# Last stage: the signs of two pairs of units are added on GpSimd, and three engines' orders are changed

## The reference, cut to what matters

```python
# h: 16384 tokens x 64; weight (1, 8, 64, 64), proj_w (8, 64), scale (1, 1, 64)
xh   = layernorm(h)
gate = (sigmoid(xh @ proj_w.T + proj_b) > 0.5)        # 8 gates, 0 or 1, per token
w    = einsum('hbe,heio->hbio', gate, weight)         # a 64 x 64 matrix per token
y    = einsum('hbi,hbio->hbo', sign(xh), sign(w))     # sum over i of sign * sign
out  = h + y * scale
```

## Time and profile before

| | |
|---|---|
| median of three runs | 1976.49 us |
| the profiled execution's own time | 1986.12 us |
| its span | 1984.3 us |
| PE busy | 1697.9 us (86%) |
| DVE busy | 1182.7 us (60%) |
| ACT busy | 975.5 us (49%) |
| POOL busy | 422.9 us (21%) |
| last stage, first sign to the end | about 1192 to 1984.3 us |

### The profile page before, as it was taken

The page is one execution under the profiler, slowest core; times in us unless marked ns, Lnnn a source line. Parts: engine busy times, 40 slices in busy tenths (PEclk is TensorE's granted clock), DMA queues, the critical chain, the costliest instruction groups (busy, mean ns, idle before and its releaser), DMA issues.

```text
span 1984.3 us, 94332 instructions
## 1 busy us (share of the span) xinstructions
PE 1697.9 (86%) x35690; PEld 1234.3 (62%) x35690; DVE 1182.7 (60%) x3445; ACT 975.5 (49%) x1765; POOL 422.9 (21%) x477
## 2 busy tenths in 40 slices
PE   5999999956568888888888779999999999999996
PEld 3566666644457666666667556666666666666663
DVE  2565656567624444444444467777777777777762
ACT  2344444423312222222222227777777777777776
POOL 2100000034322332323323222222222222222210
PEclk9899999978979999999999969999999999999998
DMA  3100000125533333333333212333333333333332
GB/s 106 36 11 13 11 11 13 32 57 104 102 86 93 92 96 94 93 96 91 97 96 92 63 33 74 79 79 79 79 79 79 79 79 79 79 79 79 79 78 57
DMA packets 254173, 141.71 MB, mean 71 GB/s; under 512 B 181314, under 2 KB 218050, under 8 KB 253858
## 3 DMA queue, kind: packets, MB, share of 16 engines
q1 hardware_dynamic: 254114, 140.88, 29.5%
HBM read 63.56 MB, written 18.42 MB: 41 GB/s over the span
## 4 chain that ended last, share of the span: by engine, by line
issue 33%; PE 29%; SPq 26%; ACT 6%; DVE 2%; DMA 2%; POOL 1%; ACTq 0%; DVEq 0%; POOLq 0%
SPq L402 13%; PE ps_D L805 8%; SPq L391 4%; ACT prob L1060 3%; PE ps_AV L822 3%; SPq L373 2%; PE ps_J L859 2%; PE ps_J L911 2%; PE ps_OT L929 2%; PE ps_J L879 2%; SPq L428 1%; PE ps_J L937 1%; PE ps_OT L954 1%; SPq L394 1%; PE ps_OT L953 1%
## 5 line engine op out<-in xcount | busy, mean ns | idle before, releaser
L1060 ACT ACTIVATE prob<-ps_D 128x1024 bf16<-128x1024 f32 x448 | 443.6, 1022 | 83.6 <-PE ps_D L805 83.2
L1231 DVE TENSOR_REDUCE m_sb<-ps_D 128x4 f32<-128x400 f32 x256 | 135.4, 571 | 207.7 <-PE ps_D L708 192.1
L1048 ACT ACTIVATE prob<-ps_D 100x512 f32<-100x512 f32 x256 | 139.0, 595 | 216.8 <-PE ps_D L730 216.8
L493 POOL TENSOR_TENSOR tile_a<-q_st,q_mask 128x1024 f32<-128x1024 f32 x64 | 123.3, 1927 | 407.5 <-DMA q_st<-q_d 369.5
L730 PE MATMUL ps_D<-tile_a,key_patch 64*100 64x128 f32 x2048 | 176.7, 288 | 0.0
L726 PE MATMUL ps_D<-mT,key_rows 64*100 64x128 bf16 x1024 | 129.3, 224 | 51.0 <-ACT mT L1037 32.2
L1184 DVE TENSOR_REDUCE top<-ps_D 128x8 f32<-128x512 f32 x128 | 79.5, 684 | 152.5 <-PE ps_D L582 152.5
L805 PE MATMUL ps_D<-tile_b,w_parts 128*128 128x256 bf16 x1024 | 155.5, 275 | 15.5 <-ACT prob L1060 9.6
L805 PE MATMUL ps_D<-tile_a,w_parts 128*128 128x256 bf16 x1024 | 156.1, 276 | 14.2 <-ACT prob L1060 9.6
L730 PEld LDWEIGHTS ps_D<-tile_a,key_patch 64*100 64x100 f32 x2048 | 146.8, 166 | 0.0
L805 PEld LDWEIGHTS ps_D<-tile_a,w_parts 128*128 128x128 bf16 x1024 | 88.5, 100 | 60.3 <-issue 47.8
(11 more groups left out here) (174 smaller groups left out, 3880.9 us busy)
## 6 DMA issues: line engine op xcount, KB each, us to landing
tile_b<-v_d SPq DMA_DIRECT2D x640, 40.0 KB
tile_a<-xg SPq DMA_DIRECT2D x384, 64.0 KB, 2.0
tile_b<-xg SPq DMA_DIRECT2D x384, 64.0 KB, 2.0
key_st<-k_d SPq DMA_DIRECT2D x64, 175.0 KB, 3.0
key_st<-k_d SPq DMA_DIRECT2D x64, 167.0 KB, 3.1
w_exp<-experts SPq DMA_DIRECT2D x64, 129.0 KB, 2.3
k_d<-kpad SPq DMA_DIRECT2D x32, 140.0 KB, 2.3
xin<-in_x SPq DMA_DIRECT2D x32, 128.0 KB, 2.3
```

The costliest lines, as they stand in the source:

```text
L493: gp.tensor_tensor(q_block[:, par, :].rearrange("c (p h q) -> c p h q", h=NH, q=NQ), q_st[:, :].rearrange("c (p a q) -> c p a q", a=1, q=N ...
L1048: act.activation(prob1[0:NKL, 2 * g + x, :], s_loc[x][0:NKL, :], ACT.Exp).then_inc(T2["exp_done"], 1)
L1060: act.activation(sgn[:, k % 4, :], unit(k, par)[:, :], ACT.Sign).then_inc(BN["sign"], 1)
L1231: dve.tensor_reduce(m_sb[:, C * x + HOT[x] + 4 * g:C * x + HOT[x] + 4 * g + 4], m_loc[x][:, 0:4 * NKL].rearrange("p (u n) -> p u n", u=4), ...
```

## The change

For each strip, POOL now adds the signs of units 2 and 3 ("fold 1") and of units 4 and 5 ("fold 2") into a new bf16 tile `fold`, and PE sums the two folded tiles in place of the four, so it sums six tiles in place of eight. Sums of two signs are -2 to 2, exact in bf16. The folds stand on POOL behind the bias addition and ahead of `rstd_ret`. The waits follow: signs 6 and 7 wait for fold 1 (they overwrite slots 2 and 3), sign 0 and the clip of the next strip wait for fold 2.

The orders change too. On PE, reduce 1 stands behind w 6, reduce 2 behind w 1 of the next pass, ahead of reduce 3, and w 3 stands ahead of L859. On ACT, sign 2 stands ahead of the first ReLU, sign 3 ahead of the second. On DVE, the clip stands first in the pass, and `ud` and `ys` stand ahead of the `xn_fg` normalisations.

```diff
@@ gpsimd, strips(j, par), between the bias addition and inv_std("ret", RT, f)
+                if q is not None:
+                    for pair in (1, 2):
+                        gp.wait_ge(BN["sign"], times(q * 7 + 2 * pair + 1))
+                        gp.wait_ge(BN["y_part"], times(q * 4 - 3 + pair))
+                        settle(gp)
+                        two = [sgn[:, k % 4, :] for k in (2 * pair, 2 * pair + 1)]
+                        gp.tensor_tensor(fold[:, pair - 1, :], two[0], two[1], ALU.add).then_inc(BN["fold"], 1)
@@ tensor, reduce(q, pair)
-                    signed(q, 2 * pair + 1)
+                    if pair in (1, 2):
+                        pe.wait_ge(BN["fold"], times(q * 2 + pair))
+                        parts = [(fold[:, pair - 1, :], 0)]
+                    else:
+                        signed(q, 2 * pair + 1)
+                        parts = [(sgn[:, k % 4, :], int(k == 1)) for k in (2 * pair, 2 * pair + 1)]
@@ tensor, order
+                    reduce(p, 2)
                     reduce(p, 3)
...
+                if q is not None:
+                    signed(q, 1)
+                    weights(3, par, unit(3, par))
...
-                    signed(q, 1)
-                    weights(3, par, unit(3, par))
                     pe.wait_ge(BN["ysum"], times(q))
                     reduce(q, 0)
...
                     weights(5, par, unit(5, par))
-                    reduce(q, 1)
...
                     weights(6, par, unit(6, par))
-                    reduce(q, 2)
+                    reduce(q, 1)
@@ scalar, sign(k)
-                    act.wait_ge(BN["y_part"], times(q * 4 + k // 2 - 1))
+                    if k in (0, 6, 7):
+                        act.wait_ge(BN["fold"], times(q * 2 + (1 if k else 0)))
+                    else:
+                        act.wait_ge(BN["y_part"], times(q * 4 + k // 4))
@@ vector, the clip, now first in the pass
-                    dve.wait_ge(BN["y_part"], times(q * 4 - 1))
+                    dve.wait_ge(BN["fold"], times(q * 2))
```

More of the change, by code:

```diff
@@ L181, in build @@
         sgn = prob1[:, :, :].bitcast(BF16)
+        fold = sb("fold", [P, 2, 1024], BF16)
         x_parts = [tile_a[:, :, :].rearrange("p a n -> p (a n)").bitcast(BF16), tile_b[:, :, :].rearrange("p a n -> p (a n)").bitcast(BF16)]
@@ L231, in build @@
         BN = named("bin", "stats", "mv", "veps", "rstd", "xn", "xs", "g_ps", "gates", "x_ps", "xg", "x_in", "w_ps", "sign", "clip",
-                   "y_part", "ysum", "y_ps", "ys", "y", "stored")
+                   "fold", "y_part", "ysum", "y_ps", "ys", "y", "stored")
         CREDIT = 4
@@ L511, in strips @@
             def strips(j, par):
-                e, f, b = (inside(j - k) for k in (0, 1, 3))
+                e, f, b, q = (inside(j - k) for k in (0, 1, 3, 6))
                 if b is not None:
@@ L817, in reduce @@
                         signed(q, 0)
-                    signed(q, 2 * pair + 1)
+                    if pair in (1, 2):
[4 more added lines that the diff above has]
+                        parts = [(sgn[:, k % 4, :], int(k == 1)) for k in (2 * pair, 2 * pair + 1)]
                     settle(pe)
-                    for k in (2 * pair, 2 * pair + 1):
+                    for n, (part, by) in enumerate(parts):
                         for cg in range(4):
-                            mm = pe.matmul(bank["AV"][32 * cg:32 * (cg + 1), 0:256], lane_sum[:, int(k == 1), :], sgn[:, k % 4, cg * 256:(cg + 1) * 256],
-                                           start=k == 0, stop=k == 7)
+                            mm = pe.matmul(bank["AV"][32 * cg:32 * (cg + 1), 0:256], lane_sum[:, by, :], part[:, cg * 256:(cg + 1) * 256],
+                                           start=pair == 0 and n == 0, stop=pair == 3 and n == 1)
                     mm.then_inc(BN["y_part"], 1)
@@ L1073, in strips @@
                     act.activation(xs[:, :], bank["T"][:, 0:256], ACT.Sign).then_inc(BN["xs"], 1)
+                if q is not None:
+                    sign(2)
                 if f is not None:
@@ L1077, in strips @@
                     act.activation(hidT[:, 0, :], bank["J1"][:, 0:256], ACT.Relu, bias=b_i[:, 0:1]).then_inc(FF["hid_sb"], 1)
-                if q is not None:
-                    sign(2)
                 if r is not None:
@@ L1083, in strips @@
                     act.activation(xrT[:, :], bank["OT"][:, 0:256], ACT.Copy).then_inc(RT["xT_sb"], 1)
+                if q is not None:
+                    sign(3)
                 if f is not None:
@@ L1088, in strips @@
                 if q is not None:
-                    sign(3)
                     sign(4)
@@ L1297, in strips @@
                 turns = min(max(j, 0), NSTRIP + 3) if isinstance(j, int) else j
+                if q is not None:
+                    dve.wait_ge(BN["w_ps"], times(q * 8 + 2))
+                    dve.wait_ge(BN["fold"], times(q * 2))
+                    dve.tensor_scalar(sgn[:, 1, :], unit(1, par)[:, :], -TINY, TINY, ALU.max, ALU.min).then_inc(BN["clip"], 1)
                 if r is not None:
@@ L1303, in strips @@
                     dve.tensor_scalar(kd3[:, 1, 0:C + 1], xn_r[:, 1, 0:C + 1], decay_k[:, :], keep[:, 0, bass.ds(r, 1)], ALU.mult, ALU.mult).then_inc(RT["kd"], 1)
-                if q is not None:
-                    dve.wait_ge(BN["w_ps"], times(q * 8 + 2))
-                    dve.wait_ge(BN["y_part"], times(q * 4 - 1))
-                    dve.tensor_scalar(sgn[:, 1, :], unit(1, par)[:, :], -TINY, TINY, ALU.max, ALU.min).then_inc(BN["clip"], 1)
                 if g is not None:
@@ L1319, in strips @@
                     moments("ffn", FF, e, row(e * 2))
-                if e is not None:
-                    normalize("ffn", FF, e, row(e * 2), lambda t: xn_fg[:, t, 0:C], FF["xT_ps"], turns)
-                if b is not None:
-                    normalize("bin", BN, b, row(b * 2), lambda t: xn_fg[:, t, C:P], FF["xT_ps"], turns)
                 if r is not None:
@@ L1333, in strips @@
                                       scale_bc[:, :].rearrange("p (a c) -> p a c", a=1).broadcast_to((P, 2, C)), ALU.mult).then_inc(BN["ys"], 1)
+                if e is not None:
+                    normalize("ffn", FF, e, row(e * 2), lambda t: xn_fg[:, t, 0:C], FF["xT_ps"], turns)
+                if b is not None:
+                    normalize("bin", BN, b, row(b * 2), lambda t: xn_fg[:, t, C:P], FF["xT_ps"], turns)
                 if g is not None:
```

## The result

The changed kernel takes 1997.32 us at the median (1993.13 to 1999.31). The kernel before, run beside it, takes 1978.38 us (1973.61 to 1981.2). The ratio is 1.0103 [1.0086, 1.012]: slower by about 20 us, where +10 was forecast. The profiled execution took 1996.97 us (span 1994.8). That of before was 8 us above its median, so the two spans differ by only 10.5 us; the last stage, from the start of its first `xg` to the end, went from 808.6 us (1175.7 to 1984.3) to 828.9 us (1165.9 to 1994.8), 20.3 us more. (Counted from the first sign it is 21.9 us, but the new order of ACT puts that sign 1.6 us nearer to the first `xg`.)

The account below looks back on a forecast made before the run. PE was taken to bound the kernel before, fold 1's loop the changed one: 12.60 us per pass against 12.43, +0.17 over 58 passes, +9.9 us, so 1986.5 us. The forecast's own range was 1975 to 2003, the stated range 1942 to 2010 us.

Parts of the forecast that it names:

- the loop closed by fold 1: PE's first FFN layer (W), DVE chain, POOL's fold 1, signs 6 and 7, w 1, next W: 12.60 us per pass.
- w 1 to W: On PE, from w 1 to the next first FFN layer, with the clip and w 3 between: 2.54 us.
- the ends of the stage: First six passes without folds and last ones without bias addition: put at 0, with 3 us to either side.
- W to fold 1's start: First FFN layer on PE, through gates, moments, `xn_fg` and bias addition, to POOL's fold 1: 5.72 us.
- D: Length of a fold on POOL, 2.1 us, low end 1.1; also the rival that the change moves nothing, within 4 us.
- fold 1's end to w 1: Sign 6 starts 0.10 after fold 1, w 1 2.08 after sign 6's start, and `yo`'s hold adds about 0.05.
- The fewer matmuls: On PE, two tiles fewer to sum save 0.33 us per pass, 21 us over 64 strips if PE alone counted.
- PE's list: PE's own work without late folds: 6.29 us from W to w 6, 11.62 us per pass.
- the hold: DVE's `yo`, with two SBUF inputs, waits inside fold 1 until W + 7.97; adds about 0.05 us per pass.
- A: Rival: PE gets its gain, as a fold takes only 1.1 to 1.5 us; 1930 to 1948 us, chance 0.20.
- B: Rival: the walk is too strict, the loop's constant is 0.3 to 0.5 us smaller; 1963 us, chance 0.15.
- C: Rival: DVE's `yo` loses to both folds on POOL, a pass takes 14.75 us; 2110 us, chance 0.10.

Follow-up runs that it names:

- e2: The changed kernel with each fold adding only 512 of 1024 columns, PE reading these twice: 1943.87 us, 0.9848 of the kernel before.
- e3: The changed kernel with `yo` reading the unscaled sums from PSUM, so one SBUF input, scale left out: 1988.10 us, 1.0069 of the kernel before.
- e4: The changed kernel with `ud` and `ys` between the two `xn_fg` on DVE: 2147.84 us, 1.0872 of the kernel before.
- e1: The changed kernel without folds, PE summing eight tiles, reduces 1 and 2 behind w 5 and w 6: 1967.14 us, 0.9962 of the kernel before.
- e12: The kernel before with only DVE's gates moved behind the retention layer's addition and both moments: 1960.26 us, 0.9915 of the kernel before.
- e8: The changed kernel with DVE's gates behind the moments and both `xn_fg` ahead of `ud` and `ys`: 1952.17 us, 0.9867 of the kernel before.
- e9: e8's order on DVE without folds, PE summing eight tiles: 1949.94 us, 0.9872 of the kernel before.
- e11: The changed kernel with DVE's gates behind the moments, `ud` still ahead of `xn_fg`, `ys` behind it, folds kept: 1954.26 us, 0.9881 of the kernel before.

## Why the prediction was right or wrong

The direction was right, the forecast's range of 1975 to 2003 us held the time, and the mechanism forecast is the one seen: the loop closed by fold 1. The size was too small, +10 us for about +20. Two terms of the sum were mis-sized: the pass, 12.60 for 12.73, most of it in the step from w 1 to W (2.54 for 2.64), and the ends of the stage, put at 0, which cost about 4 us. Term by term, two successive passes, the first from W = 1500.81 and the second from 1513.50:

| step | forecast | pass 1 | pass 2 |
|---|---|---|---|
| W to fold 1's start | 5.72 | 5.66 | 5.79 |
| D | 2.10 | 2.125 | 2.125 |
| fold 1's end to w 1 | 2.23 | 2.27 | 2.25 |
| w 1 to W | 2.54 | 2.64 | 2.65 |
| sum | 12.59 | 12.69 | 12.81 |

- **The fewer matmuls** were priced rightly: two folded tiles cost 0.23 and 0.12, which saves 0.31 of the 0.66 of reduces 1 and 2 (forecast 0.33), and under the fold's loop they are worth nothing, as forecast. PE's list had 6.29 to w 6 and took 6.44, but that is two errors that nearly cancel. The stop at L889, below, is not in the 6.29 (reduce 0 to the transpose takes 0.92, 1501.44 to 1502.36, and took 0.35 before). Against it, PE lost more before than the idle in brackets says: w 5 came 0.47 behind the start of L901 (1509.52 to 1509.99) and comes 0.06 behind the start of L917 now (1504.47 to 1504.53), so its wait was worth 0.41 and not 0.25.
- **D** was taken from the f32 rows, 2.1, and measured 2.125. e2 shows what the low end of 1.1 would have given.
- **Fold 2** was to hold sign 0 back by 0.2 to 0.3. It does not: the forecast had sign 0 due at W + 9.80, but w 0's result is there only for W + 10.33, and fold 2 ends at W + 9.91.
- **`yo`**, forecast to end at W + 7.97, ended at W + 7.93; L968 came at W + 8.70 (forecast 8.75) and w 1 at W + 10.05 (10.04). The worth of the hold, 0.05, was measured as 0.08 (e3). The Trainium skill's rule, page "SBUF — State Buffer", section "Who interferes with whom", holds for `yo` (1.32 us, 0.281 in e3). e4 extends what was made of it here: `xn_fg` was not weighed against the rule, and is held as well.
- **The step of the pass that failed is "w 1 to W".** The 0.45 for w 3 is what a group of four costs ahead of another full-array group. Ahead of a reduce or the FFN's first layer it costs more: w 6 to reduce 0.53 already in the earlier trace rows (1513.29 to 1513.82), w 3 to L865 0.52 in e1's pass (1508.06 to 1508.58), and 0.53 here. That is 0.08 of the 0.10. The sum took w 3 out of its old place at 0.54 and put it into the new one at 0.45.
- **A wait was missed.** L889 waits for DVE's `h` (0.52 and 0.62 us idle); before, w 3 and reduce 0 covered it (`h` ends at 1507.31, L873 of before starts at 1507.41). It delays L907, `ud` and so `xn_fg`, which start at W + 4.40 in pass 1 and W + 4.54 in pass 2, forecast 4.32. The claim that `ud` and `ys` fit into DVE's wait for `rstd_ffn` was wrong by 0.1 to 0.2. In pass 1 the shorter step from bias addition to fold hides it (0.45, forecast 0.59); in pass 2 it shows as the 0.07.
- **The sum.** From the first `xg` to the end the stage grew by 20.3 us, 10.4 more than forecast. From the first `xg` to the last, 63 intervals, it is 18.6 us (783.9 to 802.5). The 49 intervals from the seventh on gave 14.9 us, where 0.17 each is 8.3: this is the pass, 6.6 us of the miss. The first six gave -2.3, the last eight +6.1, and behind the last `xg` it is +1.7: 5.5 us, where the forecast had 1.6 for the nine of its 58 passes that lie there and nothing for the rest.
- **The ends were put at 0, and the last passes are the second step that failed.** Two of their intervals take 14.50 and 16.04 us (12.34 and 11.99 before). There no bias addition holds the folds back, they start ahead of `xn_fg`, and the two `xn_fg` are held by one fold each (4.18 us for 0.53), then `xg`, then w 7. The granted clock of these two intervals is 0.88 besides, and was 1.00 before. No run parts the two, but the kernels without folds have no interval like it (e1: 11.63 and 12.09).
- **PE's busy time** was to fall to 181 of 200 us and is 175.6. Per pass that is 11.18 us (175.61 x 12.73 / 200) against 11.76 before, 0.58 less where 0.33 was forecast. No records are missing: 1739 are 108 per pass, 1577 are 100, eight fewer. Where the other 0.25 went is not settled.
- **The rivals.** A fell with D. B, the walk too strict, was the opposite of what happened. C, `yo` loses to both folds, did not: wherever `yo` was held, it got through at the end of the fold in which it had started (median 1.32 us, and 2.22 where it started with the fold). Its price of 14.75 was not tested; that e4 took 15.3 us per pass, by another instruction and in part by the clock, is no measure of it. D fell.
- **What the first section of the prediction had wrong** is "PE is the engine to relieve". The kernel before was bound by the chain W, gates, `h`, moments, `rstd_ffn`, `xn_fg`, `ud`, `v`, L929, w 6, sign 6, sign 7, w 1. e12 shortens it without PE and gains 0.85%. Once it is short, PE's saving is worth 0.11 us per pass, and nothing that the times can tell (e8 against e9). The signs of it were in the trace of before: among its waits from 1300 to 1900 us stand, once per pass,

```profile
DVE xn_fg L1130 <- POOL rstd_ffn L478: 39.0, 48, 0.8
ACT v L1093 <- DVE ud L1328: 37.7, 49, 1.0
```

and both lie behind the gates.

The fastest versions that leave nothing out are e8 to e11, 1.2 to 1.3% faster than before and 2.2 to 2.3% faster than the change; the runs don't tell them apart.
